# A decoder layer on one core: six second-norm outputs split in SBUF and transposed by DMA, one VectorE branch, a short bias load, and a new written-out order

## The chip, the cores and the metric

The kernel runs on one core of one Trainium2 chip. A core has TensorE (PE: matrix products and transposes, results in PSUM), VectorE (DVE), ScalarE (ACT), GpSimd (POOL; it cannot read PSUM) and SyncE (SP, which here only issues DMAs). Each has its own instruction stream; they meet through semaphores. PSUM has eight banks of 128 partitions by 2 KB. The metric is the device time of one execution in microseconds (us), lower is better.

## The reference, cut to what matters

x and ctx are (16, 128, 256) in float32: 16 sequences of 128 tokens, 256 channels.

```python
# attention: 16 query heads, 4 key/value heads, head size 16, causal
q, k, v = x @ Wq.T + bq, x @ Wk.T + bk, x @ Wv.T + bv     # by heads
q, k = rope(rms_norm(q)) * q_gain, rope(rms_norm(k))
att = softmax(causal(q / 4 @ k.T)) @ v
x = layernorm(x + att @ Wo.T + bo)                        # norm 1
# WKV recurrence over the tokens: keys are x, values are ctx
for t in range(128):
    y[t] = (aa + exp(u + x[t]) * ctx[t]) / (bb + exp(u + x[t]))
    aa, bb = decay * aa + exp(x[t]) * ctx[t], decay * bb + exp(x[t])
x = layernorm(x + y)                                      # norm 2
# feed-forward, 1024 hidden units, weights reduced to their signs
h = relu((x @ sign(Wup).T) * up_scale)
out = layernorm(x + (h @ sign(Wdn).T) * down_scale * out_scale)   # norm 3
```

## The kernel before, in words

The 16 sequences are eight pairs (index p, 0 to 7), T = 2 sequences each; a tile holds 128 tokens in the partitions and t, channels in the free dimension, or 128 channels (c = 0, 1) in the partitions and 256 tokens beside them. Each pair passes through the same steps, each written as a small function with the pair as its argument. Every engine has a list of calls written out by hand, in which the steps of several pairs are interleaved; nothing reorders it at run time. A step first waits (`done(engine, name, p)`, `landed(...)` for a DMA) and its last instruction raises a semaphore. Extra `done(...)` lines between the calls guard the reuse of PSUM banks and SBUF buffers. The tables PJ, SC, PV, AC, WO, X1, YT, X2, UP, DN give the PSUM bank of each product, the table ON the engine of each step that can run on more than one (V is VectorE, A ScalarE, G GpSimd).

One pair goes like this (lines of the kernel before):

- **Projection** (PE, L417, and a product with the biases, L423): q, k and v in one bank per sequence. ACT squares (L923) and copies v (L929); DVE sums the squares (L1575), applies the rotation (L1605, L1612, L1619), and refines the inverse root (L1582 to L1590) that ACT starts by Ln and Exp. `scale_heads` makes the heads, `high_heads` and `low_heads` split them into a high and a low 16-bit half in `stack`, `swap_keys` completes it.
- **Rows**: pair 0's `stack` is transposed on PE (L431) and copied out by ACT (L964) and DVE (L1628); for pairs 1 to 7 SP issues a transposing DMA (L337, `head_rows`) of 12 blocks of 128 by 128.
- **Attention**: `scores` (PE, L472, L479), four exponentials (ACT, L971), `products` with v (PE, L500), back to tokens (L510), normalized by DVE (`attend_norm`, L1658, L1661), to channels (L519), output projection (L533).
- **Norms 1, 2, 3**: `residual`, `add_mixed` or `add_out`, then `moments` (DVE, L1676), 1/sqrt on POOL (`inverse_root` L1355, `root` L1361), then `normed`, either as two DVE instructions (L1691) or, behind `offsets` (DVE, L1682), as two ACT instructions (L1035).
- **WKV**: `keys` (ACT), `keys_by_context` (DVE or POOL), `scan` (DVE, L1702), `mix` (L1712), a reciprocal in log form with one refinement (`num_by_rec` L1734, `den_by_rec`, `refine` L1740), back to tokens (PE, `mixed_to_tokens`, L551).
- **Feed-forward**: norm 2's output x2 is transposed on PE (`x2_to_channels`, four 128 by 128 transposes, L560) into a bank; ACT copies its 16-bit high half (L1009) and DVE makes the low half (L1753). `ffn_up(p, n)`, n = 0 to 3, is 16 products of 256 columns with both halves (L576), `relu` is ACT's (L1019), `high_bits` (L1025) and `low_bits` (L1760) split the hidden values into halves again, `ffn_down(p, n)` (L597) multiplies them. `scale_out` (L1766) and `add_out` (L1773) end in norm 3 and `store`.

A run-time flag (all gains small) chooses a plain or a guarded version of the attention. PE loads the flag once, after `project(1)` (L612), and has both versions as two whole streams. DVE loads it once before `rope_cosines(2)` and then tests it eight times, once per pair, around a short guarded piece (`row_maxima`). The inputs take the plain way.

The biases are split into three 16-bit rows at the partitions 0, 32 and 64 (`split`: four dependent DVE instructions, L1518 to L1524). For that the bias vector is loaded into 96 partitions (`partition_broadcast(BR)`).

Of the kernel before, what the change touches and what calls it, by code (L numbers as in the profile page):

```python
# [43 lines left out]
def build(nc, x, xT, ctxT, wqkv, biases, gains, wo, decay_in, first_in, up, down, up_s, down_s, out_s,  # L44
          rope_cos, rope_sin, ident_in, out):
    with ExitStack() as ctx:
# [3 lines left out]
        def sem(name):  # L50
# [26 lines left out]
        OUT_N = 2  # L77

# [16 lines left out]
        flags = sb("flags", [128, 2], I32)  # L95
# [62 lines left out]
        x2hi = sb("x2hi", [128, NC, T, S], F16)  # L158
        x2lo = sb("x2lo", [128, NC, T, S], F16)
# [14 lines left out]
        spare = probs[0:BR, 2].rearrange("p g j s -> p (g j s)")  # L174
        bias_in = spare[:, 0:E + D]
        bias_rest = spare[:, E + D:2 * (E + D)]
# [13 lines left out]
            o3_done=1, r3_done=1, ag3=1, ve3=1, rs3=1, out_done=2, of1=2, of2=2, of3=2, msq_done=1, vy3_done=1)  # L190
# [3 lines left out]
            qn_done="GGVVGGGV",  # L194
# [34 lines left out]
        slots = dict(xT_in=XT_N, x_in=X_N, ctx_in=CTX_N, rows_in=ROWS_N, stored=OUT_N)  # L229
# [8 lines left out]
        bias_out_in = sem("bias_out_in")  # L238
        bias_out_ready = sem("bias_out_ready")
        gains_in = sem("gains_in")  # L240
# [27 lines left out]
        def done(eng, name, p, k=None):  # L268

            k = names[name] if k is None else k  # L270
            before = ON[name][:p].count(ON[name][p]) if name in ON else p
            eng.wait_ge(signal(name, p), before * names[name] + k)

        def turn(name, p):

            return p - 1 if name in ("rows_in", "xT_in") else p
# [9 lines left out]
        def hidden(p, n):  # L286

            if n in WHOLE:
                return hid[:, p % HID_N]
            if IN_SBUF[p][n]:  # L290
                return hid[:, sum(IN_SBUF[q][n] for q in range(p)) % HID_N]
            return banks[:, UP[p][n]].rearrange("p (j s) -> p j s", j=2)

        def down_of(j):

            return dn_f[:, j] if j // 2 in WHOLE else dn_sb[:, j]

        def scaled(p):

            return banks[:, DN[p]].rearrange("p (t d) -> p t d", t=T) if LAST_IN_PSUM[p] else r3[:, p % R3_N]  # L300

# [10 lines left out]
        GAINS = 7  # L312
# [8 lines left out]
        def _(sp):  # L321
# [17 lines left out]

            def store(p):  # L340
# [3 lines left out]

            for c in range(NC):
# [60 lines left out]
        def _(pe):  # L406
# [1675 lines left out]
```

## Time and profile before

| what | value |
|---|---|
| three runs | 178.32, 179.06, 180.08 us; median 179.06 |
| profiled execution | span 178.1 us, from its first instruction to its last |
| PE busy | 157.8 us, 89% |
| DVE busy | 156.5 us, 88% |
| ACT busy | 138.9 us, 78% |
| POOL busy | 83.4 us, 47% |

The page gives no total time of the profiled execution beside its span; the span lies 0.2 us under the fastest of the three runs and 0.96 us under their median. Busy time is the sum of what an engine ran. The instructions of one engine overlap, so the distance from one start to the next is shorter than a duration: a 512-wide DVE instruction lasts 0.68 us and the next starts 0.60 us after it when nothing holds it. "issue" in a row is time in which an engine waited for nothing that the profile shows.

### The profile page before, as it was taken

How to read it: one execution, taken by the hardware profiler on the slowest of the kernel's cores; microseconds unless marked ns; L12 is line 12 of the kernel's file. 1: busy time of each engine (PE TensorE's matmuls, PEld its weight loads, DVE VectorE, ACT ScalarE, POOL GpSimd, SP SyncE). 2: the span in 40 equal slices, each digit the busy share in tenths (PEclk: the TensorE clock that was granted, in tenths of full speed). 3: DMA queues.
4: the chain of work that ended last, by engine and by line, in shares of the span. 5: the costliest groups of instructions: out<-in, count | busy, mean ns of one | idle time of the engine just before them, and what ended most of it. 6: DMA issues, size and time to landing. Idle time of an engine off the chain costs nothing.

```text
span 178.1 us, 3837 instructions
## 1 busy us (share of the span) xinstructions
PE 157.8 (89%) x1388; PEld 107.8 (61%) x1388; DVE 156.5 (88%) x289; ACT 138.9 (78%) x280; POOL 83.4 (47%) x109
## 2 busy tenths in 40 slices
PE   7978769989999999999999999999969798999920
PEld 2445424545645645566886668769758687898810
DVE  1489679798789999999899999999999999999981
ACT  3745488988998889999899989696687897898700
POOL 8282601017404695020873623699679457270121
PEclk9999969999999999999999999999999999999995
DMA  5899039044709107941070310000300010001122
GB/s 175 244 320 392 5 62 209 2 92 75 249 0 95 56 2 94 212 127 48 0 151 0 75 48 2 0 4 0 118 0 4 0 59 0 36 27 61 63 79 107
DMA packets 17989, 14.65 MB, mean 82 GB/s; under 512 B 12656, under 2 KB 13616, under 8 KB 17712
## 3 DMA queue, kind: packets, MB, share of 16 engines
q1 hardware_dynamic: 17424, 13.87, 29.8%
q10 hardware_dynamic: 544, 0.50, 0.9%
q8 instruction: 13, 0.21, 0.5%
q14 instruction: 8, 0.07, 0.1%
HBM read 9.52 MB, written 2.10 MB: 65 GB/s over the span
## 4 chain that ended last, share of the span: by engine, by line
PE 48%; DVE 27%; ACT 10%; issue 8%; DMA 3%; POOL 2%; SPq 0%; POOLq 0%; DVEq 0%; ACTq 0%
PE banks L417 9%; PE banks L576 8%; PE banks L500 7%; PE banks L597 6%; PE banks L533 5%; DVE hid_lo L1760 5%; DVE state L1702 4%; PE banks L472 4%; ACT probs L971 3%; DMA probs<-biases_dram 3%; DVE ratio L1712 2%; DVE stats L1676 2%; PE banks L510 2%; ACT dn_sb L918 2%; PE banks L479 2%
## 5 line engine op out<-in xcount | busy, mean ns | idle before, releaser
L971 ACT ACTIVATE probs<-banks 128x1024 f32<-128x1024 f32 x32 | 31.8, 1022 | 4.8 <-PE banks L479 4.8
L597 PE MATMUL banks<-dn_sb,hid_hi 128*128 128x256 bf16 x128 | 29.1, 272 | 1.1 <-DVE hid_lo L1760 1.1
L576 PE MATMUL banks<-x2hi,up_sb 128*128 128x256 f16 x128 | 29.1, 273 | 0.8 <-DVE x2lo L1753 0.5
L597 PE MATMUL banks<-dn_sb,hid_lo 128*128 128x256 bf16 x128 | 29.1, 273 | 0.0
L576 PE MATMUL banks<-x2lo,up_sb 128*128 128x256 f16 x128 | 29.0, 272 | 0.0
L417 PE MATMUL banks<-wqkv_sb,xT_sb 128*128 128x384 f32 x64 | 23.5, 512 | 2.0 <-issue 1.6
L1355 POOL TENSOR_SCALAR veps<-stats 128x2 f32<-128x2 f32 x24 | 9.4, 394 | 27.8 <-DVE stats L1676 26.8
L1361 POOL TENSOR_TENSOR rstd<-veps,half_neg 128x2 f32<-128x2 f32 x24 | 20.4, 853 | 1.3
L1019 ACT ACTIVATE banks<-banks,ups_man 128x256 f32<-128x256 f32 x48 | 19.6, 470 | 1.8 <-PE banks L576 1.6
L417 PEld LDWEIGHTS banks<-wqkv_sb,xT_sb 128*128 128x128 f32 x64 | 12.4, 201 | 11.9 <-issue 3.4
L1702 DVE TENSOR_TENSOR_SCAN state<-dec_sb,ke 128x1032 f32<-128x1032 f32 x8 | 18.4, 2301 | 0.0
L500 PE MATMUL banks<-probs,v_sb 128*32 128x512 f32 x128 | 17.6, 632 | 0.2
L576 PEld LDWEIGHTS banks<-x2hi,up_sb 128*128 128x128 f16 x128 | 12.5, 98 | 6.0 <-issue 3.8
L1760 DVE TENSOR_TENSOR hid_lo<-banks,hid_hi 128x512 f16<-128x512 f32 x24 | 16.0, 679 | 0.0
L1025 ACT ACTIVATE hid_hi<-banks 128x512 f16<-128x512 f32 x24 | 14.3, 616 | 1.7 <-PE banks L597 0.8
L533 PE MATMUL banks<-wo_sb,attT_sb 128*128 128x256 f32 x64 | 15.1, 379 | 0.0
L597 PEld LDWEIGHTS banks<-dn_sb,hid_hi 128*128 128x128 f16 x128 | 12.5, 98 | 3.4 <-issue 1.8
L597 PEld LDWEIGHTS banks<-dn_sb,hid_lo 128*128 128x128 f16 x128 | 12.5, 98 | 1.5
L576 PEld LDWEIGHTS banks<-x2lo,up_sb 128*128 128x128 f16 x128 | 12.5, 98 | 1.4
L533 PEld LDWEIGHTS banks<-wo_sb,attT_sb 128*128 128x128 f32 x64 | 12.2, 190 | 1.5
L472 PE MATMUL banks<-rows 32*128 32x512 f16 x128 | 10.2, 394 | 3.2 <-ACT probs L971 1.5
L1405 POOL TENSOR_TENSOR hid_lo<-hid,hid_hi 128x512 f16<-128x512 f32 x5 | 5.8, 1168 | 14.7 <-ACT hid_hi L1025 14.6
(129 smaller groups left out, 355.8 us busy)
## 6 DMA issues: line engine op xcount, KB each, us to landing
ctxT_sb<-ctxT_dram SPq DMA_DIRECT2D x8, 256.0 KB, 3.1
x_sb<-x_dram SPq DMA_DIRECT2D x8, 256.0 KB, 3.8
out_dram<-outb SPq DMA_DIRECT2D x8, 256.0 KB, 2.2
xT_sb<-xT_dram SPq DMA_DIRECT2D x7, 256.0 KB, 4.4
up_f<-up_dram SPq DMA_DIRECT2D x1, 1024.0 KB, 6.4
dn_f<-down_dram SPq DMA_DIRECT2D x1, 1024.0 KB, 8.4
wqkv_sb<-wqkv_dram ACTq DMA_DIRECT2D x2, 192.0 KB, 3.1
xT_sb<-xT_dram SPq DMA_DIRECT2D x2, 128.0 KB, 2.9
```

What stands on the lines that cost most here:

```text
L417: nc.tensor.matmul(banks[:, b + t, 0:E], xT_sb[:, p % XT_N, c, t, :], wqkv_sb[:, c, :], start=(c == 0), stop=False)
L472: nc.tensor.matmul(banks[:, b[g]], q[r:r + VW, kb, :], q[r:r + VW, HB * t:HB * t + REP, :].rearrange("p j s -> p (j s)"), start=(k == 0), ...
L500: nc.tensor.matmul(banks[r:r + VW, PV[p][t], :], v_sb[:, p % V_N, t, g, :], probs[:, (T * p + t) % PROBS_N, g].rearrange("p j s -> p (j s) ...
L533: mm = nc.tensor.matmul(banks[:, WO[p], t * D:(t + 1) * D], attT_sb[:, c, t, :], wo_sb[:, c, :], start=False, stop=(t == T - 1 and c == NC ...
L576: mm = nc.tensor.matmul(banks[:, UP[p][n], s * T * S:(s + 1) * T * S], up_sb[:, c, j * 128:(j + 1) * 128], part[:, c, :, :].rearrange("p t ...
L597: mm = nc.tensor.matmul(banks[:, DN[p], t * D:(t + 1) * D], part[:, t * S:(t + 1) * S], down_of(j), start=(j == 0 and t == 0 and m == 0), ...
L971: nc.scalar.activation(probs[:, (T * p + t) % PROBS_N, 2 * h:2 * h + 2].rearrange("p n j s -> p n (j s)"), banks[:, b:b + 2], ACT.Exp).the ...
L1019: nc.scalar.activation(hidden(p, n)[:, s], banks[:, UP[p][n], s * T * S:(s + 1) * T * S], ACT.Relu, scale=ups_man[:, j:j + 1]).then_inc(se ...
L1025: nc.scalar.activation(hid_hi[:, 2 * n:2 * n + 2], hidden(p, n), ACT.Copy)\
L1361: nc.gpsimd.tensor_tensor(rstd[n][:, p % MV_N], veps[n][:, p % MV_N], half_neg[:], ALU.pow)\
L1702: nc.vector.tensor_tensor_scan(state[:, 1:2 * W + 1], dec_sb[:].rearrange("p c a t s -> p (c a t s)"), ke[:, p % KE_N].rearrange("p c a t ...
L1760: nc.vector.tensor_tensor(hid_lo[:, 2 * n:2 * n + 2], hidden(p, n), hid_hi[:, 2 * n:2 * n + 2], ALU.subtract).then_inc(signal(f"lo{n}_done ...
```

## The change

- **x2 of pairs 0 to 5** is no longer transposed on PE. ACT (POOL for pair 1) rounds it to its high half in SBUF, DVE (POOL for pair 3) makes the low half, both in token layout in `x2h`, and SP issues one transposing DMA of 8 blocks of 128 by 128 (`x2_rows`) that fills `x2T`. Pairs 6 and 7 keep the transposes on PE. `ffn_up` waits for the transfer.
- **DVE** has, like PE, one branch with two whole streams behind it in place of eight tests.
- **Biases**: three rows are loaded instead of 96 into a cleared buffer, one load for all 640 values; DVE splits the output biases too, which POOL did. The gains' load moves from ACT's queue to SP's.
- **Orders, engines, banks**: all lists are written anew. `project(2)` stands ahead of PE's branch, `project(4)` ahead of the first scores. Of norm 1's, 2's and 3's outputs, ACT makes 5, 5 and 5 (before 0, 8 and 0). POOL makes seven of the hidden values' high halves. Fourteen of the 32 hidden tiles go to SBUF (before 8).
- **End**: the last pair's feed-forward output has a bank per sequence, its last products, scaling and addition go by sequence, and it is stored in two halves.

```diff
...
-        x2hi = sb("x2hi", [128, NC, T, S], F16)
-        x2lo = sb("x2lo", [128, NC, T, S], F16)
+        x2h = sb("x2h", [128, X2H_N, 2, T, NC, 128], F16)
+        x2T = sb("x2T", [128, X2T_N, 2, T, NC, S], F16)
...
-            hi_done="AGGGGAGA",
-            lo_done="VGVVGGGG",
-            stack_done="AVAAAAAA",
-            kv_done="VGVVGVGG",
-            newt_done="GGGVGGVG",
-            guess_done="VVVGGVGV",
...
+            guess_done="GVVGGGGV",
+            hi0_done="AAAGAAAA",
+            hi1_done="AAGAAAGA",
+            hi2_done="AAGAAGAA",
+            hi3_done="AAAAGAGA",
+            hi_done="GGGGGAGG",
+            kv_done="VGGVGVVV",
...
+            lo_done="GGGGVGGG",
+            newt_done="VVGGVGVV",
+            out_done="VAVAAAAV",
...
+            stack_done="AVAVAAAA",
+            x1_done="VVAAVAAA",
+            x2_done="VAAAVAAV",
+            x2hi_done="AGAAAAAA",
+            x2lo_done="VVVGVVVV")
...
+        X2_BY_DMA = (1, 1, 1, 1, 1, 1, 0, 0)
...
+        NORM_ON_ACT = ((0, 0, 1, 1, 0, 1, 1, 1), (0, 1, 1, 1, 0, 1, 1, 0), (0, 1, 0, 1, 1, 1, 1, 0))
+        HID = ((-1, -1, 1, -1), (-1, -1, -1, -1), (0, 1, 0, -1), (0, 1, -1, -1), (-1, 0, -1, 0), (-1, 1, 0, 1), (-1, 1, -1, 0), (1, -1, -1, -1))
...
+            def x2_rows(p):
+
+                done(sp, "x2lo_done", p)
+                sp.dma_start_transpose(x2T[:, p % X2T_N].rearrange("p a t c s -> p (a t c) s"),
+                                       x2h[:, p % X2H_N].rearrange("p a t c d -> p (a t c d)")).then_inc(arrival("x2_in", p), 16)
...
-            sp.dma_start(bias_in[:, 0:E], biases[0:E].partition_broadcast(BR)).then_inc(bias_in_done, 16)
+            sp.wait_ge(bias_clear, 1)
+            sp.dma_start(bias_in[0:BR:32], biases.partition_broadcast(3)).then_inc(bias_in_done, 16)
+            for dst, src in gain_loads:
+                sp.dma_start(dst, src).then_inc(gains_in, 16)
...
             def ffn_up(p, n):
 
-                if n == 0:
-                    done(pe, "x2hi_done", p)
-                    if p == 0:
-                        pe.wait_ge(up_ready, 1)
-                done(pe, "x2lo_done", p)
+                if X2_BY_DMA[p]:
+                    landed(pe, "x2_in", p)
+                else:
+                    done(pe, "x2lo_done", p)
...
             project(0)
             project(1)
-            pe.wait_ge(masks_ready, MASKS)
-            pe.wait_ge(guard_ready, GUARDS)
+            project(2)
             pe.wait_ge(gain_ready, GAINS)
             plain = pe.value_load(flags[0:1, 0:1], min_val=0, max_val=1)
...
+                mixed_to_tokens(5)
                 ffn_up(3, 0)
+                done(pe, "z_done", 5)
+                x1_to_channels(6)
                 ffn_up(3, 1)
-                done(pe, "r1_done", 7)
                 ffn_up(3, 2)
-                mixed_to_tokens(5)
-                done(pe, "hid_done", 3, 6)
-                ffn_up(3, 3)
-                x1_to_channels(6)
-                x2_to_channels(4)
-                x1_to_channels(7)
-                done(pe, "ek_done", 6)
                 ffn_down(3, 0)
+                x1_to_channels(7)
+                ffn_up(3, 3)
+                done(pe, "ek_done", 7)
                 ffn_up(4, 0)
...
                 ffn_down(7, 2)
-                ffn_down(7, 3)
+                ffn_down_half(7, 0)
+                ffn_down_half(7, 1)
...
             def high_x2(p):
 
-                done(act, "x2T_tr", p)
-                nc.scalar.activation(x2hi[:].rearrange("p c t s -> p (c t s)"), banks[:, X2[p]], ACT.Copy)\
-                    .then_inc(sems["x2hi_done"], 1)
+                if X2_BY_DMA[p]:
+                    done(act, "x2_done", p)
+                    nc.scalar.activation(x2h[:, p % X2H_N, 0].rearrange("p t c d -> p (t c d)"),
+                                         x2[:, p % X2_N].rearrange("p t d -> p (t d)"), ACT.Copy)\
+                        .then_inc(signal("x2hi_done", p), 1)
...
                 relu(7, 2)
...
+                landed(act, "stored", 2)
+                normed(2, 4)
                 high_bits(7, 2)
                 relu(7, 3)
...
                 high_bits(7, 3)
+                landed(act, "stored", 3)
+                normed(2, 5)
+                landed(act, "stored", 4)
+                normed(2, 6)
...
                 done(dve, "x2hi_done", p)
-                nc.vector.tensor_tensor(x2lo[:].rearrange("p c t s -> p (c t s)"), banks[:, X2[p]],
-                                        x2hi[:].rearrange("p c t s -> p (c t s)"), ALU.subtract)\
-                    .then_inc(sems["x2lo_done"], 1)
+                if X2_BY_DMA[p]:
+                    high, low = [x2h[:, p % X2H_N, part].rearrange("p t c d -> p (t c d)") for part in range(2)]
+                    whole = x2[:, p % X2_N].rearrange("p t d -> p (t d)")
+                else:
+                    high, low, whole = x2_part(p, 0), x2_part(p, 1), banks[:, X2[p]]
+                nc.vector.tensor_tensor(low, whole, high, ALU.subtract).then_inc(signal("x2lo_done", p), 1)
...
+            nc.vector.memset(bias_in, 0.0).then_inc(bias_clear, 1)
...
             split_biases()
             gains_constants()
...
+            plain = dve.value_load(flags[0:1, 0:1], min_val=0, max_val=1)
+
+            def from_heads(guarded):
+
+                split_out_biases()
+                rope_sines(0)
+                head_sums(0)
...
+                add_mixed(5)
+                moments(0, 7)
+                normed(1, 4)
+                moments(1, 5)
+                moments(2, 2)
+                low_x2(4)
...
+            with dve.If(plain):
+                from_heads(False)
+            with dve.Else():
+                from_heads(True)
```

Three places show the order. In each, of before first, then of the change. The first is PE's beginning, from its branch to the first scores: L417 and L454 are the projections, L423 and L460 their biases, L431 and L468 the transposes of pair 0's rows, L472 and L515 scores.

```order
L417 MATMUL banks<-wqkv_sb,xT_sb 128x384 x4
L423 MATMUL banks<-bias_rows,ones_b 128x384 x2
L612 TENSOR_LOAD flags
L612 ISA x2
L869 COMPARE_AND_BRANCH
L417 MATMUL banks<-wqkv_sb,xT_sb 128x384 x4
L423 MATMUL banks<-bias_rows,ones_b 128x384 x2
L417 MATMUL banks<-wqkv_sb,xT_sb 128x384 x4
L423 MATMUL banks<-bias_rows,ones_b 128x384 x2
L431 MATMUL banks<-id_h,stack 128x128 x12
L472 MATMUL banks<-rows 128x512 x8
```

```order
L454 MATMUL banks<-wqkv_sb,xT_sb 128x384 x4
L460 MATMUL banks<-bias_rows,ones_b 128x384 x2
L665 TENSOR_LOAD flags
L665 ISA x2
L892 COMPARE_AND_BRANCH
L454 MATMUL banks<-wqkv_sb,xT_sb 128x384 x4
L460 MATMUL banks<-bias_rows,ones_b 128x384 x2
L468 MATMUL banks<-id_h,stack 128x128 x12
L454 MATMUL banks<-wqkv_sb,xT_sb 128x384 x4
L460 MATMUL banks<-bias_rows,ones_b 128x384 x2
L515 MATMUL banks<-rows 128x512 x8
```

Three projections stand ahead of the load of the flag instead of two, and a fifth projection stands between the transposes of pair 0 and its scores.

The second place is DVE around the low half of pair 4's x2 (the last row of each). `z` is the sum ahead of norm 2 (its row is pair 5's in both), `stats` are moments, L1691 and L1713 norm outputs.

```order
L1691 TENSOR_SCALAR x<-r,stats,rstd 128x256 x2
L1747 TENSOR_TENSOR z<-x,banks 128x512
L1691 TENSOR_SCALAR x<-r,stats,rstd 128x256 x2
L1676 BN_STATS stats<-z 128x6
L1760 TENSOR_TENSOR hid_lo<-banks,hid_hi 128x512
L1753 TENSOR_TENSOR x2lo<-banks,x2hi 128x512
```

```order
L1769 TENSOR_TENSOR z<-x,banks 128x512
L1698 BN_STATS stats<-r 128x6
L1713 TENSOR_SCALAR x<-z,stats,rstd 128x256 x2
L1698 BN_STATS stats<-z 128x6
L1698 BN_STATS stats<-r 128x6
L1780 TENSOR_TENSOR x2h<-x,x2h 128x512
```

The low half is made from x2 and x2h in SBUF instead of from the bank; between pair 5's z and it stand the moments of norm 1 (pair 7), pair 4's norm 2 output, and two more moments.

The third place is DVE's end: `hid_lo` are low halves of hidden values, L1766, L1791 and L1804 the scaling, L1773, L1798 and L1809 the addition, `outb` the output.

```order
L1760 TENSOR_TENSOR hid_lo<-banks,hid_hi 128x512
L1760 TENSOR_TENSOR hid_lo<-hid,hid_hi 128x512
L1773 TENSOR_TENSOR r<-r,x 128x512
L1760 TENSOR_TENSOR hid_lo<-banks,hid_hi 128x512
L1691 TENSOR_SCALAR outb<-r,stats,rstd 128x256 x2
L1676 BN_STATS stats<-r 128x6
L1766 TENSOR_TENSOR banks<-banks,dsc_b 128x512
L1773 TENSOR_TENSOR r<-banks,x 128x512
L1691 TENSOR_SCALAR outb<-r,stats,rstd 128x256 x2
L1676 BN_STATS stats<-r 128x6
L1691 TENSOR_SCALAR outb<-r,stats,rstd 128x256 x2
```

```order
L1785 TENSOR_TENSOR hid_lo<-banks,hid_hi 128x512
L1704 SCALAR_TENSOR_TENSOR offset<-stats,rstd 128x2
L1798 TENSOR_TENSOR r<-r,x 128x512
L1785 TENSOR_TENSOR hid_lo<-banks,hid_hi 128x512
L1698 BN_STATS stats<-r 128x6
L1804 TENSOR_TENSOR banks<-banks,dsc_b 128x256
L1809 TENSOR_TENSOR r<-banks,x 128x256
L1804 TENSOR_TENSOR banks<-banks,dsc_b 128x256
L1809 TENSOR_TENSOR r<-banks,x 128x256
L1704 SCALAR_TENSOR_TENSOR offset<-stats,rstd 128x2
L1698 BN_STATS stats<-r 128x6
L1713 TENSOR_SCALAR outb<-r,stats,rstd 128x256 x2
```

One norm output (pair 6) has left the end, replaced by its offset, and the last pair's scaling and addition stand as two halves each.

## Rows read from the trace of the kernel before

**Rows 1.** The page: busy time and share of the span, shares of the chain.

```profile
PE 157.8 (89%) x1388; PEld 107.8 (61%) x1388; DVE 156.5 (88%) x289; ACT 138.9 (78%) x280; POOL 83.4 (47%) x109
...
PE 48%; DVE 27%; ACT 10%; issue 8%; DMA 3%; POOL 2%; SPq 0%; POOLq 0%; DVEq 0%; ACTq 0%
```

**Rows 2.** Four stretches: length, busy us of PE, PEld, DVE, ACT, POOL; clock; DMA.

```profile
24.00:26.00 2.00, 1.90 (x28) 0.93 (x32) 1.83 (x5) 1.23 (x3) 0.00 (x0) 0.51 0.27 53
26.00:28.00 2.00, 2.00 (x10) 0.51 (x3) 1.05 (x5) 2.00 (x4) 0.00 (x0) 0.64 1.21 97
130.00:140.00 10.00, 8.07 (x71) 6.73 (x70) 9.96 (x17) 7.92 (x19) 6.72 (x7) 1.00 0.01 2
160.00:170.00 10.00, 10.00 (x94) 8.81 (x93) 9.13 (x18) 7.69 (x17) 1.17 (x3) 1.00 0.15 56
```

**Rows 3.** The chain of waits, beginning: start us, us, what.

```profile
1.64 5.29 DMA probs<-biases_dram
...
9.42 2.58 PE banks L417 x8
...
12.33 1.59 issue
```

**Rows 4.** Timeline of PE, ACT, DVE: start, us, instruction, idle before it and releaser.

```profile
8.92 0.50 PE L423 MATMUL banks<-bias_rows,ones_b 96*128 96x384 bf16 x2 [0.35 <-DVE bias_rows L1524]
...
21.78 0.61 PE L472 MATMUL banks<-rows 32*128 32x512 f16 x8 [1.12 <-ACT rows L964]
...
24.10 1.04 PE L472 MATMUL banks<-rows 32*128 32x512 f16 x8 [1.48 <-ACT probs L971]
...
42.28 0.61 PE L472 MATMUL banks<-rows 32*128 32x512 f16 x8
...
26.72 1.01 ACT L971 ACTIVATE probs<-banks 128x1024 f32<-128x1024 f32 x1
...
22.30 0.83 DVE L1612 TENSOR_TENSOR banks<-banks,cos_sb 128x640 f32<-128x640 f32 x1 [0.45 <-issue]
```

**Rows 5.** Groups by line: instruction, count, busy us, mean ns, idle before.

```profile
L971 ACT ACTIVATE probs<-banks 128x1024 f32<-128x1024 f32 x32 | 31.8, 1022 | 4.8 <-PE banks L479 4.8
L1691 DVE TENSOR_SCALAR x<-r,stats,rstd 128x256 f32<-128x256 f32 x16 | 6.5, 454 | 0.7 <-POOL rstd L1361 0.7
L1753 DVE TENSOR_TENSOR x2lo<-banks,x2hi 128x512 f16<-128x512 f32 x8 | 5.4, 677 | 0.6 <-ACT x2hi L1009 0.6
L1009 ACT ACTIVATE x2hi<-banks 128x512 f16<-128x512 f32 x8 | 4.8, 596 | 2.8 <-PE banks L560 2.6 <-PE banks L576 0.2
```

**Rows 6.** Transfers into the tile rows (seven transposing DMAs): time to landing.

```profile
DMA to landing us min/median/max: 3.6/4.3/5.3
```

**Rows 7.** The chain of waits from 152 us to the end.

```profile
152.13 0.45 PE banks L560 x4
...
158.66 0.87 PE banks L576 x8
...
169.27 0.65 DVE outb L1691 x2
169.92 0.61 DVE stats L1676
170.53 0.67 DVE banks L1766
...
171.29 0.42 DVE r L1773
...
172.63 0.62 DVE stats L1676
...
174.88 0.32 DVEq L46
```

**Rows 8.** Two lines alone: count, shortest, median and longest ns, first and last start.

```profile
L1734 DVE TENSOR_TENSOR ratio<-ratio,rec x5: 672/766/1725, 59.6 to 151.5; 128x512 f32<-128x512 f32 x5
...
L1361 POOL TENSOR_TENSOR rstd<-veps,half_neg x24: 688/699/2682, 46.0 to 173.7; 128x2 f32<-128x2 f32 x24
```

More of the change, by code:

```diff
@@ L270, in done @@
             k = names[name] if k is None else k
-            before = ON[name][:p].count(ON[name][p]) if name in ON else p
+            before = ON[name][:p].count(ON[name][p]) if name in ON else turn(name, p)
             eng.wait_ge(signal(name, p), before * names[name] + k)
         def turn(name, p):
+            if name == "x2T_tr":
+                return X2_BY_DMA[:p].count(0)
+            if name in ("of1", "of2", "of3"):
+                return sum(NORM_ON_ACT[int(name[2]) - 1][:p])
             return p - 1 if name in ("rows_in", "xT_in") else p
@@ L286, in hidden, with x2_part, down_tile @@
         def hidden(p, n):
[L288 to L291, printed above, removed]
+            if HID[p][n] >= 0:
+                return hid[:, HID[p][n]]
             return banks[:, UP[p][n]].rearrange("p (j s) -> p j s", j=2)
[L294 to L300, printed above, removed]
+        def x2_part(p, part):
+            return x2T[:, p % X2T_N, part].rearrange("p t c s -> p (t c s)")
+        def down_tile(p, t):
+            if p == PAIRS - 1:
+                return banks[:, DN[p] + t, 0:D]
+            return banks[:, DN[p], t * D:(t + 1) * D]
         def alone(eng):
@@ L400, in _ @@
             store(6)
-            store(7)
-            for p in range(PAIRS - OUT_N, PAIRS):
-                landed(sp, "stored", p)
+            store_half(7, 0)
+            store_half(7, 1)
+            landed(sp, "stored", PAIRS - 3)
+            landed(sp, "stored", PAIRS - 2)
+            sp.wait_ge(last_stored, 16 * T)
         @block.tensor
@@ L679, in from_scores @@
                 products(3, 0)
+                products(3, 1)
                 done(pe, "r1_done", 2)
-                done(pe, "probs_done", 3)
                 if guarded:
@@ L1509, in _, with split @@
         def _(dve):
-            nc.vector.memset(ones_b[:], 0.0).then_inc(bias_ones, 1)
-            dve.wait_ge(bias_ones, 1)
-            for r in (0, 32, 64):
-                nc.vector.memset(ones_b[r:r + 1], 1.0).then_inc(bias_ones, 1)
-            def split(a, b, landing, ready):
-                dve.wait_ge(landing, 16)
+            def split(a, b, ready):
                 nc.vector.tensor_copy(bias_rows[:, a:b], bias_in[:, a:b]).then_inc(ready, 1)
@@ L1672, in moments @@
             def moments(n, p):
-                done(dve, ("r1_done", "z_done", "r3_done")[n], p)
+                done(dve, ("r1_done", "z_done", "r3_done")[n], p, T if n == 2 and p == PAIRS - 1 else None)
                 rows_of = (r1[:, p % R1_N], z[:, p % Z_N], r3[:, p % R3_N])[n]
```

1176 lines of the change are left out of this document (579 added, 597 removed).

## The prediction

> **What bounds the kernel now.** I read the page's busy times and chain shares first [rows 1]: PE is busy 89% of the span, DVE 88%, ACT 78%, and the chain that ended last runs through PE for 48% and DVE for 27%. No engine is the bound everywhere, so I went on by stretches [rows 2]. From 130 to 140 us DVE is busy 9.96 of 10 us and PE 8.07; from 160 to 170 us PE is busy all ten and DVE 9.13. Up to about 100 us PE leads with short waits, then DVE to 150, then PE to its last product at 170.5, then a serial end on DVE [rows 7]. A change that only relieves one engine therefore gives little; what counts is work taken off PE and DVE alike, waits at the beginning, and the end.
>
> The sum is against the profiled span of 178.1 us; the runs' median, 179.06, lies 0.96 above, and I carry the difference in microseconds over to it.
>
> **The beginning, -1.8.** The bias load takes 5.29 us from 1.64 us [rows 3] and four dependent DVE instructions follow, so that PE's bias products wait 0.35 us until 8.92 [rows 4]. With three rows the load should land earlier; no row shows so small a bias load, so it is worth nothing to the whole 0.35, since from then on PE's own products are last. I take 0.35: the wait is shorter than any plausible shortening of a 5.29 us load. The clearing memset falls under SP's first two issues, which also end near 1.6 us.
>
> A projection with its biases takes 12.33 - 9.42 = 2.91 us [rows 3]. PE's new order ends the first at 9.42 - 0.35 = 9.07, the third at 14.9, pays the same 1.59 us for loading and testing the flag [rows 3] (16.5), ends the fourth at 19.4, transposes pair 0's rows, and does the fifth to about 23.2. So scores(0,0) start near 23.2 instead of 21.78. In return the fifth projection is out of the way, and PE no longer idles 1.12 and 1.48 us around there [rows 4]. After those two idle stretches the granted clock is 0.51 from 24 to 26 us and 0.64 from 26 to 28 [rows 2]: the 1.2 GHz level for most of these four microseconds, worth about 2 x 0.49 + 2 x 0.36 = 1.7 us.
>
> ACT then sets the pace: its four exponentials of pair 0 (1.02 us each [rows 5]) run from about 24.5 to 28.5. Before, the fourth ended at 26.72 + 1.01 = 27.73 and scores(2,0) began at 42.28 [rows 4], 14.55 us later, with the fifth projection between. Without its 2.91 us that is 11.64, so scores(2,0) could begin at 28.5 + 11.64 = 40.1; I take 40.5, as part of the freed time becomes waits for ACT. PE has done the same calls by then in both lists. 42.28 - 40.5 = **1.8** gained. Bounds: all of the idle time, the clock and the bias wait together would be 0.35 + 2.6 + 1.7 = 4.65 gained; everything simply following the later first scores would be 1.4 lost.
>
> DVE's branch: its flag load and test cost 0.45 us of "issue" at 22.30 before [rows 4]; PE's, with a long alternative behind it as DVE now has, 1.59. It now sits before the first rotation, with the output biases' four instructions behind it (under the 1.9 us of the larger split). I take 0.45, the row of the same engine; it is then covered by the wait for ACT's squares. At 1.59 the first rotation is about 1 us late and PE's fourth projection, which waits for the rotation's bank, absorbs it until 16.5. The seven later tests show no gap on DVE before, so their removal is worth nothing.
>
> **Transposes off PE, -2.6.** Four transposes hold PE 0.45 us [rows 7]; six pairs make 2.6. That counts because PE is the late engine before and after the DVE stretch.
>
> **DVE and ACT, no term of their own.** DVE makes nine norm outputs instead of sixteen; a pair of instructions takes 0.65 us from start to start [rows 7], so 4.55 leave, and seven more offsets, the output biases and the moved half-products give back about 1.3: some 3 us off 156.5. It must fall by about as much as PE, or PE waits for it; it does. ACT gets seven more norms but seven fewer high halves and is busy 78% [rows 1]; its total changes by about 1 us.
>
> **The transfers, +2.1.** Pair by pair, 0.45 us of PE transposes and ACT's copy out of the bank (0.60) [rows 5, 7] are replaced by a trip through SP, while the high and low halves are made ahead of it at the old price (0.60 and 0.68 [rows 5]). No row shows a transfer of 8 blocks; those of 12 landed 3.6 to 5.3 us after issue [rows 6]. By size the bounds are two thirds of 3.6, 2.4 us, and the longest, 5.3; I take 3.6, the shortest seen, since part of a trip does not shrink. So x2 reaches PE about 2.5 us later per pair, 15 us if every microsecond were exposed, nothing if PE always has other work.
>
> The Trainium skill, page "VectorE: DVE Perf Modes", section "The three transpose paths", gives 1309 ns for one 128x128 block by DMA against 390 ns on TensorE, and its rules prefer TensorE where PSUM is a possible destination. Eight blocks in a row would by that be an estimated 10.5 us, and pair 4 alone would wait about 9; the seven transfers here speak against it, with 12 blocks in 3.6 to 5.3 us.
>
> Where is it exposed? The order shows the closest place at pair 4. Behind pair 5's mixed_to_tokens, DVE has z, three moments, a norm output and the low half: five 0.60 steps and one of 0.65, 3.7 us, then the trip of 3.6: 7.3. PE meanwhile has four ffn_up and one ffn_down at 0.87 [rows 7] and two groups of transposes at 0.45: 5.2. The wait is **2.1** us, 0.9 to 3.8 with the trip's bounds. Pairs 3 and 5 have over 7 us of products between; for 0 to 2 I assume attention work covers the trip.
>
> **The end, -1.3.** From PE's last product to the end of the span took 7.6 us. Now the first sequence's scaling and addition run beside the last products; a half of each is left, saving about 0.3 + 0.3, pair 6's norm output (0.65 [rows 7]) moves to ACT, leaving an offset, and the last store is half as large, worth 0 to 0.6, taken as 0.3 plus nothing else: 1.6 with rounding. Against that ACT has a norm output of pair 4 ahead of high_bits(7,2), which I walk as 0.3 us late at the last half products. The last moments, the root on POOL and the store's trip stay.
>
> **Sum:** -1.8 - 2.6 - 1.3 + 2.1 = -3.6: span 174.5, median **175.5 us**.
>
> **The rivals.** Within 1% (177.27 to 180.85) counts as no change, about what the spread of the three runs can tell.
> - *The transfers sit on the path* (12%, slower). Pairs 0, 1, 2 and 4 each expose the trip: three more pairs at 2.5 give 183.0. For it: x2 was used by PE almost as soon as DVE had it, and SP issues in order. Against: the lists move ffn_up behind attention work. It turns slower by over 1% when PE waits 5.4 us more than I allow, two full trips.
> - *DVE and POOL get in each other's way* (14%, no change). On DVE, twelve more instructions read two tiles of SBUF (five low halves of x2, seven more of hidden values), and POOL has more to do. One such instruction took 1.73 us and not 0.67, and a POOL root 2.68 and not 0.69 [rows 8]. At the mean excess of that line, 0.26 us, twelve cost 3.1 and the time is 178.6; at 1.05 each, 12.6. The Trainium skill, page "SBUF — State Buffer", section "Who interferes with whom", states an exclusive lock between a DVE instruction with two SBUF inputs and a GpSimd one that reads SBUF; the two long rows agree, the medians in the same rows say that it is rare.
> - *The beginning gains nothing* (8%, no change): DVE's branch costs 1.59, the first scores stay late, and 1.8 + 1.1 are lost: 178.4.
> - *Everything is hidden* (20%, faster): no wait at pair 4, and up to 1 us more of the clock's 1.7: 172.4.
> - The forecast has 46%.
>
> Faster by over 1%: 0.46 + 0.20 = 0.66; within 1%: 0.22; slower: 0.12. The range takes in the hidden case with another 1.4 for the beginning's upper bound, 171.0, and the two cases of no change with part of the slow one, 180.0.
>
> **What will show it.** Granted clock 1.00 from 24 to 28 us and scores(2,0) at 40 to 41 us; the eight-block transfers landing in 2.4 to 4.3 us; PE's wait ahead of the up products of pair 4 about 2 us, and small ones ahead of pairs 0 to 2; PE's last product 6.3 us before the end; the L1734 kind of DVE row near 0.67. Waits of 2 us and more ahead of several pairs' first up products, or long rows on DVE beside POOL's, would make it wrong.

## The result, and the profile after

The changed kernel takes 183.27 us (median of 4 runs, 182.72 to 184.56), the kernel before beside it 178.69 (4 runs): the ratio is 1.025, 95% interval 1.018 to 1.032. The forecast was 175.5 in a range of 171 to 180, so sign and range are both missed. That the first rival had named 183.0 is luck: the experiments show that its mechanism isn't the cause.

The page's busy times and chain shares come first; [rows 1] are their counterpart.

```profile
PE 152.8 (84%) x1364; PEld 104.6 (58%) x1364; DVE 161.8 (89%) x289; ACT 140.6 (78%) x282; POOL 95.8 (53%) x116
...
DVE 41%; PE 18%; issue 10%; ACT 6%; POOL 6%; DMA 5%; POOLq 0%; DVEq 0%
```

PE lost 5.0 us of work, 2.6 of them the transposes. DVE, with the same 289 instructions, is busy 5.3 us *longer*, and leads the chain with 41% where PE had 48%. The stretches that answer to [rows 2] (same columns):

```profile
24.00:26.00 2.00, 1.35 (x32) 0.65 (x32) 1.22 (x5) 1.59 (x4) 0.00 (x0) 1.00 0.47 90
26.00:28.00 2.00, 0.89 (x12) 0.16 (x8) 0.95 (x2) 2.00 (x4) 1.73 (x2) 1.00 1.22 171
130.00:140.00 10.00, 7.49 (x65) 6.16 (x66) 9.41 (x17) 8.44 (x19) 7.92 (x7) 1.00 0.12 28
160.00:170.00 10.00, 9.67 (x89) 8.49 (x88) 8.15 (x15) 8.52 (x20) 2.84 (x6) 1.00 0.01 2
```

The clock is at 1.00 from 24 to 28 us, as forecast. Where DVE's time went shows when its rows are laid beside POOL's. The timeline of both (start, us, engine, line, instruction, count, idle before and its releaser), first DVE, then POOL:

```profile
107.90 2.32 DVE L1734 SCALAR_TENSOR_TENSOR ratio<-ke,now_gain,state 128x512 f32<-128x512 f32 x2
...
111.41 1.68 DVE L1713 TENSOR_SCALAR outb<-r,stats,rstd 128x256 f32<-128x256 f32 x2
...
122.34 1.64 DVE L1785 TENSOR_TENSOR hid_lo<-hid,hid_hi 128x512 f16<-128x512 f32 x1
...
126.69 1.21 DVE L1704 SCALAR_TENSOR_TENSOR offset<-stats,rstd 128x2 f32<-128x2 f32 x1
...
108.25 1.42 POOL L1417 TENSOR_TENSOR hid_lo<-hid,hid_hi 128x512 f16<-128x512 f32 x1 [0.47 <-ACT hid_hi L1050]
111.62 1.32 POOL L1394 TENSOR_TENSOR ratio<-ratio,rec 128x512 f32<-128x512 f32 x1 [1.95 <-ACT rec L1024]
...
122.27 1.17 POOL L1406 TENSOR_TENSOR x2h<-x,x2h 128x512 f16<-128x512 f32 x1
...
126.61 1.27 POOL L1394 TENSOR_TENSOR ratio<-ratio,rec 128x512 f32<-128x512 f32 x1
```

Each long DVE row overlaps a wide POOL row and ends a fixed time after it, a little less than its own usual time: the low half at 122.34 ends at 123.98, 0.54 us after POOL's 123.44 (usually it takes 0.68), the mix 0.55, the norm output 0.15; the offset, 128 by 2 elements and usually 0.15 us, waits through nearly a whole POOL product and ends 0.02 us after it. Twelve DVE calls are over the median of the same call in the two kernels by about 9 us in all (before: about 2). POOL's own excess is about 17 us (before: about 10).

The small constants at the beginning are such a case too, at 0.35 and 0.17 us before:

```profile
35.30 1.43 DVE L1577 TENSOR_SCALAR dsc_b<-dsc_b,osc_b 128x256 f32<-128x256 f32 x1
36.76 1.25 DVE L1579 TENSOR_SCALAR u_rest<-u_clip 128x2 f32<-128x2 f32 x1
...
35.30 1.28 POOL L1362 TENSOR_TENSOR qn<-rot,rscale 128x640 f32<-128x640 f32 x1 [2.61 <-DVE rscale L1612]
36.53 1.45 POOL L1375 TENSOR_TENSOR stack<-qn,stack 128x640 f16<-128x640 f32 x1
```

The transfers, by contrast, hardly show. Of the tile x2T: duration and landing (ns, then us); and two rows of PE's waits (total us, times, longest):

```profile
L356 SPq DMA_TRANSPOSE x2T<-x2h x6: 1232/1234/1239, 73.2 to 142.2; - x6
...
DMA to landing us min/median/max: 2.7/2.8/4.5
```

```profile
PE banks L641 <- DVE hid_lo L1785: 7.0, 6, 2.0
...
PE banks L620 <- DMA x2T<-x2h: 0.5, 1, 0.5
```

PE waits 0.5 us for transfers in all, and 7.0 us, in six waits ahead of down products, for DVE's low halves. The end, in the chain of waits (start, us, what), answers to [rows 7]:

```profile
173.03 0.45 PE banks L653 x4
...
173.50 0.44 DVE banks L1804
...
175.18 0.15 DVE offset L1704
175.33 0.68 DVE stats L1698
...
177.56 0.41 DVE outb L1713
```

From PE's last product (173.9) to the end of the span at 181.3 it still takes 7.4 us.

### The profile page after: what moved, and what is told of

It reads as the page before. It is cut to its first block, busy times and chain, and to the rows that moved or that the text cites. A ratio compares the mean times of both kernels' runs of the same rounds, so it can differ in the third digit from the quotient of the medians.

```text
span 181.3 us, 3762 instructions
## 1 busy us (share of the span) xinstructions
PE 152.8 (84%) x1364; PEld 104.6 (58%) x1364; DVE 161.8 (89%) x289; ACT 140.6 (78%) x282; POOL 95.8 (53%) x116
## 4 chain that ended last, share of the span: by engine, by line
DVE 41%; PE 18%; issue 10%; ACT 6%; POOL 6%; DMA 5%; POOLq 0%; DVEq 0%
PE banks L641 7%; PE banks L620 5%; DVE state L1724 5%; DVE ratio L1734 4%; DVE stats L1698 4%; DVE hid_lo L1785 4%; DMA rows<-stack 3%; DVE ny L1762 3%; POOL rstd L1355 3%; DMA x2T<-x2h 2%; DVE r L1691 2%; PE banks L543 2%; ACT probs L991 2%; DVE z L1769 2%; PE banks L454 2%
## 5 line engine op out<-in xcount | busy, mean ns | idle before, releaser
L620 PE MATMUL banks<-x2T,up_sb 128*128 128x256 f16 x256 | 32.4, 273 | 0.7 <-DMA x2T<-x2h 0.5
L620 PEld LDWEIGHTS banks<-x2T,up_sb 128*128 128x128 f16 x256 | 24.4, 98 | 8.1 <-issue 2.5
L1355 POOL TENSOR_TENSOR rstd<-veps,half_neg 128x2 f32<-128x2 f32 x24 | 24.1, 1005 | 1.5
L454 PE MATMUL banks<-wqkv_sb,xT_sb 128*128 128x384 f32 x64 | 22.8, 500 | 0.6 <-ACT probs L991 0.6
L1394 POOL TENSOR_TENSOR ratio<-ratio,rec 128x512 f32<-128x512 f32 x5 | 8.2, 1637 | 20.4 <-ACT rec L1024 20.3
L543 PE MATMUL banks<-probs,v_sb 128*32 128x512 f32 x128 | 16.6, 603 | 2.7 <-ACT probs L991 2.7
L454 PEld LDWEIGHTS banks<-wqkv_sb,xT_sb 128*128 128x128 f32 x64 | 12.2, 196 | 8.4 <-ACT probs L991 1.3
L1044 ACT ACTIVATE banks<-banks,ups_man 128x256 f32<-128x256 f32 x36 | 14.7, 452 | 1.1 <-PE banks L620 0.9
L1362 POOL TENSOR_TENSOR qn<-rot,rscale 128x640 f32<-128x640 f32 x6 | 7.7, 1278 | 14.8 <-DVE rscale L1612 14.8
L1044 ACT ACTIVATE hid<-banks,ups_man 128x256 f32<-128x256 f32 x28 | 11.8, 478 | 2.8 <-PE banks L620 1.6
L515 PE MATMUL banks<-rows 32*128 32x512 f16 x128 | 9.8, 379 | 4.4 <-DVE z L1769 1.6
L1734 DVE SCALAR_TENSOR_TENSOR ratio<-ke,now_gain,state 128x512 f32<-128x512 f32 x16 | 13.0, 853 | 0.1
L1785 DVE TENSOR_TENSOR hid_lo<-banks,hid_hi 128x512 f16<-128x512 f32 x18 | 12.0, 678 | 0.3 <-ACT hid_hi L1050 0.3
```

The source lines that it names most:

```text
L454: nc.tensor.matmul(banks[:, b + t, 0:E], xT_sb[:, p % XT_N, c, t, :], wqkv_sb[:, c, :], start=(c == 0), stop=False)
L515: nc.tensor.matmul(banks[:, b[g]], q[r:r + VW, kb, :], q[r:r + VW, HB * t:HB * t + REP, :].rearrange("p j s -> p (j s)"), start=(k == 0), ...
L543: nc.tensor.matmul(banks[r:r + VW, PV[p][t], :], v_sb[:, p % V_N, t, g, :], probs[:, (T * p + t) % PROBS_N, g].rearrange("p j s -> p (j s) ...
L620: mm = nc.tensor.matmul(banks[:, UP[p][n], s * T * S:(s + 1) * T * S] .rearrange("p (t s) -> p t s", t=T), up_sb[:, c, j * 128:(j + 1) * 1 ...
L1044: nc.scalar.activation(hidden(p, n)[:, s], banks[:, UP[p][n], s * T * S:(s + 1) * T * S], ACT.Relu, scale=ups_man[:, j:j + 1]).then_inc(se ...
L1355: nc.gpsimd.tensor_tensor(rstd[n][:, p % MV_N], veps[n][:, p % MV_N], half_neg[:], ALU.pow)\
```

## The experiments

Three theories stood against each other. Theory 1: a DVE instruction with two inputs in SBUF (or one that scales or copies SBUF to SBUF) and a POOL instruction that reads SBUF exclude each other, and the new order makes more of them meet with POOL first. Theory 2: the transfers' trip is on the path. Theory 3: POOL has more to do and answers late. Each ratio compares with the kernel before in the same session. The changed kernel was timed in one session only, and the medians of the kernel before differ by up to 0.8 us between sessions (178.54 to 179.30), so a run's distance from 183.27 is uncertain by about that much.

**POOL that only writes.** 27 wide POOL calls become fills:

```diff
-nc.gpsimd.tensor_tensor(hid_lo[:, 2*n:2*n+2], hidden(p, n), hid_hi[:, 2*n:2*n+2], ALU.subtract)
+twice(hid_lo[:, 2*n:2*n+2])        # two memsets in a row; copies become one
 ...
```

> The changed kernel with GpSimd's 27 wide calls outside the heads (products with context and reciprocal, high and low halves, one high and one low half of x2, the output's additions) turned into fills that read nothing: a tensor operation becomes two fills of its output in a row, a copy one. The results of these 27 calls are left out. GpSimd stays busy for about as long (two fills of 128x512 some 1.1 us, against 1.16 to 1.4). Theory 1 (VectorE's instructions with two tiles of SBUF and GpSimd's reads exclude each other): VectorE's long rows (12 calls, 8.9 us over their usual time) mostly go, VectorE's busy time falls from 161.8 to about 156, the time from 183.3 to 177 to 179. Theory 2 (the transfers' trip is on the path) and theory 3 (GpSimd answers late because it has more to do): VectorE's rows stay and the time stays at 182 to 184.

180.19 us, ratio 1.003 (0.999 to 1.007). Its busy times, and then groups by line (count, busy us, mean ns), for the mix, the low half from SBUF and the offset; behind them the same three in the changed kernel:

```profile
PE 153.1 (86%) x1364; PEld 104.8 (59%) x1364; DVE 156.0 (87%) x289; ACT 140.2 (78%) x282; POOL 83.2 (47%) x135
```

```profile
L1741 DVE SCALAR_TENSOR_TENSOR ratio<-ke,now_gain,state 128x512 f32<-128x512 f32 x16 | 11.3, 745 | 0.1
...
L1792 DVE TENSOR_TENSOR hid_lo<-hid,hid_hi 128x512 f16<-128x512 f32 x10 | 6.8, 681 | 0.3 <-ACT hid_hi L1052 0.3
...
L1711 DVE SCALAR_TENSOR_TENSOR offset<-stats,rstd 128x2 f32<-128x2 f32 x15 | 2.3, 156 | 1.4 <-POOL rstd L1364 1.2
```

```profile
L1734 DVE SCALAR_TENSOR_TENSOR ratio<-ke,now_gain,state 128x512 f32<-128x512 f32 x16 | 13.0, 853 | 0.1
...
L1785 DVE TENSOR_TENSOR hid_lo<-hid,hid_hi 128x512 f16<-128x512 f32 x10 | 8.1, 814 | 0.3 <-ACT hid_hi L1050 0.3
...
L1704 DVE SCALAR_TENSOR_TENSOR offset<-stats,rstd 128x2 f32<-128x2 f32 x15 | 3.4, 227 | 1.4 <-POOL rstd L1355 1.2
```

DVE's 5.8 us are gone, and every long row after 81 us. The time fell by 3.1, less than the 4 to 6 expected: PE's last product is 4.2 us earlier, at 169.7, but the last norm output then waits 1.68 us until the store of pair 5, whose buffer it takes, has landed. POOL was busy 83 and not 96 us, so this alone doesn't exclude theory 3; the run with waits below does.

**No trip.** PE reads x2h untransposed; SP only waits. Since PE now reads x2h, ACT's rounding of a later pair also waits for the up products two pairs back:

```diff
-            x2_rows(0)
+            done(sp, "x2lo_done", 0)      # and so for pairs 1 to 5
 ...
-                    landed(pe, "x2_in", p)
+                done(pe, "x2lo_done", p)
```

> The changed kernel without the six transposing transfers of x2: TensorE reads the halves untransposed from x2h as soon as VectorE has made the low one, and SyncE only waits where it issued. Left out is the transposition of six pairs. Theory 1: the trip costs what TensorE's waits ahead of the first up products show, 0.5 us and little more: 182 to 183.5. Theory 2: 2.1 us (the wait at pair 4 that the forecast charged) to 6 (the trip exposed at several pairs) come off: 177 to 181. Theory 3: no change.

182.94 us, ratio 1.017 (1.008 to 1.026): 0.3 us under the changed kernel, no difference that can be told (the two intervals of the ratio overlap). The trace agrees: DVE is busy 161.6, its long rows are the same twelve, and PE waits 7.0 us for low halves, as in the changed kernel. Theory 2 falls.

**Only the transfers, in the order of before.** x2 as in the change, six `x2_to_channels` dropped, six `x2_rows` put where SP stood idle.

> The kernel before with only the six pairs' x2 halved in SBUF and transposed by transfers; orders, engines, banks and all else as before. TensorE loses six groups of transposes, 2.6 us. Theory 1: six more VectorE instructions with two tiles of SBUF, about one us of collisions, and in this order little between low half and up products: 178 to 181. Theory 2: each pair's up products wait for the trip (2.8 us) since the order has no cover: slower than before by 4 to 10 us, 183 to 189. Theory 3: no statement.

201.87 us, ratio 1.122 (1.112 to 1.133), beyond all expectations. PE's longest wait, and two stretches behind such waits (columns of [rows 2]):

```profile
PE banks L589 <- DMA x2T<-x2h: 16.2, 6, 3.5
```

```profile
79.00:82.50 3.50, 3.49 (x17) 2.62 (x18) 3.50 (x4) 1.60 (x3) 0.31 (x1) 0.52 0.39 131
...
104.00:107.50 3.50, 3.50 (x20) 2.17 (x23) 2.47 (x4) 0.81 (x2) 2.19 (x3) 0.50 0.49 149
```

Six waits, 2.7 us on average, are 16.2 of the span's 22 lost. Behind the two shown (waits of 1.96 and 2.78 us) PE runs at 0.50 to 0.52, the 1.2 GHz level, through the next up products; not behind each, since after a third, of 2.04 us, the granted clock is 1.00 (117.2 to 119.2 us) and 16 up products take 1.92 us. The trip is expensive wherever nothing covers it; the change's new order covers it, and that part of the forecast held. The run says something on theory 1 too: with six more instructions of two SBUF tiles on DVE, but in the order of before, only five DVE calls are long, by about 4 us in all, and one of them is a low half of x2. So the number of such instructions alone doesn't make the 9 us; the new order does, as far as this much slower run can be compared.

**High halves back to ACT.** All seven of POOL's `high_bits` go behind ACT's relu.

> The changed kernel with GpSimd's seven high halves of hidden values (0.92 us each with waits) back on ScalarE, right behind the relu that they split. Theory 1: one of VectorE's long rows (the low half at 122.3, 0.96 us over) and part of two more go with them, and 6.5 us of GpSimd's reads: 180.5 to 182.5. Theory 2: no change, 183 to 184. Theory 3: GpSimd has 6.5 us less to do and its roots come earlier: 181 to 182.5.

182.81 us, ratio 1.017 (1.007 to 1.027). DVE is busy 158.8 us, 3.0 less, yet the time fell by 0.5 only. PE still waits 5.1 us for low halves, probably since ACT (busy 144.1) makes the high ones later in its queue; that isn't shown. The run doesn't tell the theories apart.

**Small constants one call earlier.**

```diff
                 attend_norm(0)
+                small_constants()
                 newton_rms(4)
-                small_constants()
```

> The changed kernel with VectorE's six small constants moved one call up, ahead of the Newton step of pair 4, whose result releases GpSimd's two long calls on the heads. At their old place two of the six took 1.43 and 1.25 us (the same kind takes 0.35 and 0.17 before). Theory 1 (mutual exclusion): both come down to their usual time, VectorE's call to about 1.2 us and not 3.3, residual(0) about 1 us earlier than 38.86, the time 0.5 to 1.5 us less: 181.8 to 182.8. Theory 2 (the long rows belong to these instructions themselves, and only theory 3's late GpSimd counts): no change.

182.00 us, ratio 1.020 (1.014 to 1.026), 1.3 under the change; the intervals overlap, so the size is uncertain. The trace shows the step itself: the two instructions take 0.34 and 0.17 us now, residual(0) starts at 38.02 instead of 38.86, and scores(2,0) at 40.48 instead of 41.27.

**POOL waits for DVE.** Nothing but seven waits, such as

```diff
+            done(pool, "ratio_done", 4)
             low_bits(2, 0)
 ...
+            done(pool, "of3", 1)
             num_by_rec(5)
```

> The changed kernel with seven waits more on GpSimd and nothing else: seven of its wide calls (low heads of pair 7, context product 4, low half (2,0), numerator 4, high half (2,1), low half of x2 of pair 3, numerator 5) start only when the VectorE call is done with which they collided at 80.9, 99.2, 107.9, 111.4, 114.9, 122.3 and 126.7. GpSimd only gets later by it. Theory 1: VectorE's long rows at these seven places go, 6.3 us, and the time falls by 2 to 5 us: 178.3 to 181.3. Theory 3 (GpSimd answers late): the time rises, 183.5 to 186.

179.60 us, ratio 1.005 (1.002 to 1.009): 3.7 us *faster* than the change by making an engine wait. The same places of the timeline:

```profile
107.08 1.41 DVE L1741 SCALAR_TENSOR_TENSOR ratio<-ke,now_gain,state 128x512 f32<-128x512 f32 x2
...
119.58 0.68 DVE L1792 TENSOR_TENSOR hid_lo<-hid,hid_hi 128x512 f16<-128x512 f32 x1
...
122.97 0.15 DVE L1711 SCALAR_TENSOR_TENSOR offset<-stats,rstd 128x2 f32<-128x2 f32 x1
...
108.58 1.16 POOL L1417 TENSOR_TENSOR hid_lo<-hid,hid_hi 128x512 f16<-128x512 f32 x1 [1.60 <-DVE ratio L1741]
```

2.32, 1.64 and 1.21 us became 1.41, 0.68 and 0.15, and DVE is busy 156.9 us, 4.9 less. Theory 3 said slower and falls; theory 1 is shown. One collision only moved: POOL's low heads of pair 7 now block mix(2) for 1.25 us.

**Both edits, with one last store, with two halves, and two edits more.**

> The two edits before together, and the last pair stored by one transfer and not two. Theory 1: the two gains add up, and the end, where the second store was issued 0.43 us after the first, gets 0.2 to 0.5 us shorter: 176.5 to 180, about even with the kernel before or ahead of it. Theory 3: 183 to 186.

177.94 us, ratio 0.996 (0.992 to 1.000).

> The changed kernel with the small constants earlier and the seven waits on GpSimd, and the last pair's store in halves as the change has it. Theory 1: the gains of the two edits alone (1.3 and 3.7 us) add up to about 178.3 from 183.3; and the single store cost time (its last transfer took 4.1 us after the last norm output, the halves 3.3), so 0.5 to 1 us less than the three edits' 177.94: 176.8 to 177.6. If the single store was the gain and not a loss: 178.2 to 178.8.

177.71 us, ratio 0.995 (0.992 to 0.999). The two gains add up (5.0) and a little more; whether the last store is one or two can't be told from these medians, and I had expected 0.5 us.

> As the kernel with both edits, and two more of the same: GpSimd's low heads of pair 7 wait for mix(2) (which they now blocked for 1.25 us) and not for the refinement ahead of it; and the high half (3,0) goes from GpSimd to ScalarE, so that the root of pair 5's second norm starts before VectorE's chain of two-tile instructions that held it for 3.8 us. Theory 1: another 1 to 2 us off, 175.3 to 176.8. If VectorE's order at that place sets the time and not the root: 176.5 to 177.3.

177.00 us, ratio 0.990 (0.987 to 0.994), the fastest here and ahead of both kernels. In the chain of the changed kernel pair 5's root took 3.84 us; here, in the timeline, its usual time:

```profile
134.90 3.84 POOL rstd L1355
```

```profile
127.25 0.69 POOL L1356 TENSOR_TENSOR rstd<-veps,half_neg 128x2 f32<-128x2 f32 x1
```

It gained 0.7 and not 1 to 2 us: PE's waits for low halves stay at 4.7 us, so DVE's order there, more than the root, seems to count, as the second expectation had it.

**The last moments first.** On top of both edits, `moments(2, 7)` ahead of `offsets(2, 6)`.

> As the kernel with both edits, with the last moments one instruction ahead of the offset of pair 6, which stands 0.31 us of issue and 0.15 us in their way. If the last chain through moments, root and norm output sets the end: 0.2 to 0.5 us less. If the store of pair 6, which is issued ahead of the last pair's and now comes later, holds the last stores up: no change or 0.1 to 0.6 us more.

178.73 us, ratio 0.999 (0.994 to 1.003): 1.0 slower than with both edits alone. Its chain of waits runs through a store:

```profile
167.53 4.30 DMA out_dram<-outb
```

The last norm output waits until 171.83 for that store (pair 5), and pair 6's store is issued later, right ahead of the last two. How much of the 1.0 us that is stays open: in the two profiled executions PE's last product already ends at 168.5 instead of 168.1, which the edit doesn't touch.

**The same waits in the kernel before.** Two of them.

> The kernel before with two such waits on GpSimd: the denominator of pair 0 and the output's addition of pair 0 start only when VectorE's numerator 0 and norm output (0,3) are done, which they blocked at 59.6 and 93.2 (1.04 and 0.80 us over). Theory 1: both rows come down to 0.69 and 0.81, VectorE is 1.8 us shorter, and since TensorE leads up to 100 us there, 0 to 1.5 us of it show: 177.5 to 179.3. If the collisions cost nothing as long as TensorE leads: no change.

180.36 us, ratio 1.011 (1.006 to 1.015): slower, against both expectations. The two calls are short now, but others met POOL in their place, among them the next norm output, (0,4), which is 0.95 us over; the timeline of DVE and POOL has two more:

```profile
58.65 1.17 DVE L1584 TENSOR_TENSOR ysq<-y 128x40 f32<-128x40 f32 x1 [0.23 <-ACT y L943]
...
67.77 1.08 DVE L1684 SCALAR_TENSOR_TENSOR offset<-stats,rstd 128x2 f32<-128x2 f32 x1
...
58.49 1.27 POOL L1395 TENSOR_TENSOR newt<-ratio,rec 128x512 f32<-128x512 f32 x1 [0.81 <-DVE ratio L1736]
...
67.74 1.10 POOL L1389 TENSOR_TENSOR ke<-ke,ctxT_sb 128x512 f32<-128x512 f32 x1 [0.17 <-ACT ke L992]
```

DVE's excess is about 1 us larger than in the kernel before, not smaller. The profiled execution was the fastest of six, so where the median's 1.8 us went stays open.

**Two engines alone.** Eight stages, DVE's eight instructions of a kind beside POOL's products (POOL is idle in the first and fills in the third). This kernel ran once.


> A kernel of its own that computes nothing of the reference: in eight stages VectorE runs eight instructions of one kind while GpSimd runs four products of two SBUF tiles of 128x512 (none in stage 1, eight fills in stage 3). Theory 1: halves of a tile with both inputs in SBUF take 0.68 us alone and beside fills, and up to a whole GpSimd call more (1.3 to 2 us) beside products; with one input in PSUM 0.68 us throughout; the statistics stay at 0.69; the 128x2 and 128x256 scalings and the copy, with one input in SBUF, can be blocked as the small constants were. Theory 2 and 3: the same durations in all stages of a kind.

The timeline, DVE's row of each of the eight stages in their order, and POOL's of the second and the fifth:

```profile
10.03 4.89 DVE L94 TENSOR_TENSOR got_h<-b,half 128x512 f16<-128x512 f32 x8
...
14.99 6.27 POOL L121 TENSOR_TENSOR other<-a,b 128x512 f32<-128x512 f32 x4 [14.55 <-DVE got_h L94]
15.56 8.65 DVE L94 TENSOR_TENSOR got_h<-b,half 128x512 f16<-128x512 f32 x8
...
24.87 4.89 DVE L94 TENSOR_TENSOR got_h<-b,half 128x512 f16<-128x512 f32 x8
...
30.41 4.86 DVE L96 TENSOR_TENSOR got_h<-banks,half 128x512 f16<-128x512 f32 x8
...
35.35 4.92 POOL L121 TENSOR_TENSOR other<-a,b 128x512 f32<-128x512 f32 x4 [0.58 <-DVE got_h L96]
35.92 4.45 DVE L98 TENSOR_SCALAR got_s<-small 128x2 f32<-128x2 f32 x8
...
41.02 5.93 DVE L100 TENSOR_SCALAR got<-a,small 128x256 f32<-128x256 f32 x8
...
47.60 4.88 DVE L102 BATCH_NORM_STATS2 got_s<-a 128x6 f32<-128x512 f32 x8
...
53.13 6.51 DVE L104 CAST got_h<-a 128x512 f16<-128x512 f32 x8
```

Two inputs in SBUF: 4.89 us alone and beside fills, 8.65 beside products. One input in PSUM: 4.86 beside the same products; statistics: 4.88. Eight scalings of 128 by 2 took 4.45 us, until POOL's four products (4.92 us) were over; in the kernels such a one takes 0.16 or 0.17 us when nothing holds it. The copies took 6.51 us for eight, where a single one ahead of the stages took 0.36, so they are held up too, and the scalings of 128 by 256 likewise (5.93 for eight).

The Trainium skill, page "SBUF — State Buffer", section "Who interferes with whom", states just this: a DVE instruction with two SBUF inputs meets a GpSimd one that reads SBUF, not one that only writes, and copies and scalings with a single SBUF input can as well, in their two-port modes; whoever is first keeps the shared ports for the whole instruction, and the other is blocked. These stages agree: 8.65 us against 4.89, 4.86 and 4.88.

## Why the prediction was wrong

**The step that failed** is "DVE and ACT, no term of their own". It put DVE's busy time "some 3 us off 156.5" and went on: "It must fall by about as much as PE, or PE waits for it; it does." It rose by 5.3 us to 161.8, since meetings with POOL made DVE's calls about 9 us longer than usual (before: about 2), and PE waited for the low halves. The sum had these meetings at nothing; they stood only in the second rival, at 14% and 178.6.

That rival had the right mechanism and too small a price: "At the mean excess of that line, 0.26 us, twelve cost 3.1". Two things were wrong in it. A mean over five rows, of which one is far over, tells how often they met in the old order and not how much a meeting costs; it costs DVE nearly the rest of the POOL instruction that is ahead, 0.35 to 1.14 us here. And I counted only the twelve *new* two-tile instructions, while most of the losers are of other kinds: mix, refine, the norm outputs, the small constants, the offset of 128 by 2 (of which DVE has seven more, not counted either). They lost because the new order lets POOL start just ahead of them: waits on POOL alone give 3.7 us back.

**DVE's work.** The work itself fell about as worked out: with most collisions gone (the run with two edits more) DVE is busy 154.0, 2.5 below the kernel before. So the condition was the right one, and the collisions broke it.

**Transposes off PE, -2.6.** They left PE's busy time, but from 50 to 150 us DVE is busy 9.4 to 10.0 of every 10 us, and PE's waits for low halves rose from 1.1 to 7.0 us.

**Transfers, +2.1.** Too much: 0.5 us, at pair 1 and none at pair 4. (The row of 0.87 us is a whole `ffn_up`, 8 products and not 16 as the description has it, so that sum was right.) The landing, 2.7 to 4.5 us with a median of 2.8 where 3.6 was taken, lay in the bounds of 2.4 to 5.3. The rival that gave 183.0 is refuted in its mechanism.

**The beginning, -1.8.** scores(2,0) began at 41.27, 1.0 earlier. The rest went into the small constants that POOL blocked: with them moved it begins at 40.48, as forecast. The clock came to 1.00, but by luck. PE still idles 1.26 us ahead of the transposes of pair 0's rows and 1.63 us here:

```profile
24.65 0.61 PE L515 MATMUL banks<-rows 32*128 32x512 f16 x8 [1.63 <-ACT probs L991]
```

And the kernel with two waits, with the order of before in this place and the same idle stretches of 1.12 and 1.48 us, shows 1.00 at 24 to 28 us as well. I took one profiled execution's dip for the kernel's.

**The end, -1.3.** It gained 0.2. The halves did pull the last moments to 1.4 us behind PE's last product (2.1 before), but an offset stands ahead of them (its 0.31 us of issue and 0.15 us were not in the sum), two stores are issued in place of one, and beside it runs a chain that I had not seen: pair 5's norm output on ACT until 172.9, its store, then the last norm output, at 177.23, in the same buffer. In the runs with moments first and with the filling POOL that store is what the last norm output waits for.

**Sum.** With most collisions out of the way, the change does gain a little: 177.71 and 177.00 us, 0.995 and 0.990 of the kernel before, where the forecast was 175.5. Of the 7.8 us between forecast and result, both edits give back 5.6; what the remaining 2.2 are made of isn't accounted for term by term.

## What to carry to other kernels

Lay VectorE's and GpSimd's rows side by side and ask of each pair of neighbours whether both read SBUF, and who starts first; price a meeting at the rest of the first one's instruction, even for an operand of 128 by 2. On an engine that bounds a stretch it can pay to make the other engine wait, but look at what it then meets instead. A number that a rival hits is no proof of its mechanism: take that mechanism away and time it.

## What the runs showed of the hardware that was not expected

- The blocked side can starve over several instructions: POOL's root of 128 by 2, usually 0.69 us, took 3.84 us from 134.90, while DVE ran a product, a low half and a scan back to back, each with two tiles in SBUF, until 138.25.
- A blocked DVE instruction ends a fixed time after the POOL instruction that blocks it, in the changed kernel 0.54 to 0.55 us for 128 by 512, 0.14 to 0.15 for 128 by 256 and 0.02 for 128 by 2; that is 0.13 to 0.25 less than its usual time.
- Waits for transfers can cost more than their length: behind waits of 1.96 and 2.78 us PE ran on at a granted 0.52 and 0.50 for the next up products; behind another, of 2.04 us, it stayed at 1.00.
- A transposing transfer of 8 blocks lands in 2.7 to 2.8 us as a rule, one of 12 in 3.6 at the least [rows 6].
